# A graph layer on one core: VectorE normalises the second row tile and a small turn order at the end is changed

## What is computed

```python
h = relu(layernorm(x))                      # per row
xn = batchnorm(h) * norm1_g + norm1_b       # per column
agg = segment_sum(xn[src], dst) / max(deg, 1)
conv_out = relu(agg @ W_conv + b_conv)
q, k, v = heads(h_dense, Wq), heads(h_dense, Wk), heads(h_dense, Wv)   # the first 256 rows, 8 heads
attn = linear_attention(phi(q), phi(k), v)  # random features with exp
h_attn = (attn @ Wo)[pos]                   # rows past 255 take the last row
y = conv_out + h_attn + h
out = x + batchnorm(y) * norm2_g + norm2_b
```

## Time and profile before

| What | Value |
|---|---|
| Median of three executions | 176.18 us (175.99 to 176.76) |
| Profiled execution, its time | 176.07 us |
| Profiled execution, its span | 174.2 us |
| PE busy | 165.6 us (95%) |
| DVE busy | 137.9 us (79%) |
| ACT busy | 89.9 us (52%) |
| HBM read / written | 10.92 MB / 2.56 MB |

### The profile page before, as it was taken

How to read it: one execution, slowest core, us unless ns; L and a number is a source line. 1 busy time by engine, 2 the same in 40 slices (tenths; PEclk the granted TensorE clock), 3 DMA queues, 4 the chain that set the end, 5 groups by cost and what they waited for, 6 DMA issues and landing times.

```text
span 174.2 us, 3024 instructions
## 1 busy us (share of the span) xinstructions
PE 165.6 (95%) x1131; PEld 108.9 (63%) x1132; DVE 137.9 (79%) x315; ACT 89.9 (52%) x163; POOL 7.6 (4%) x22
## 2 busy tenths in 40 slices
PE   7899999999999999999999999999999999999960
PEld 2388877545545546557777798684464574767940
DVE  2868889989947786999656785975999998597981
ACT  3426999839694779979416164217600505004050
POOL 5037000000000000000000000000000000000000
PEclk9999999999999999999999999999999999999998
DMA  5997970000610000000000000000294014050046
GB/s 186 362 328 185 346 261 0 0 4 0 218 43 0 4 0 0 0 4 2 0 4 0 0 4 0 0 4 4 70 336 186 0 28 119 6 147 0 4 124 172
DMA packets 11884, 13.71 MB, mean 79 GB/s; under 512 B 1458, under 2 KB 6748, under 8 KB 11868
## 3 DMA queue, kind: packets, MB, share of 16 engines
q1 hardware_dynamic: 10476, 12.13, 21.3%
q10 hardware_dynamic: 1072, 1.10, 1.8%
q0 software_dynamic: 320, 0.26, 0.7%
HBM read 10.92 MB, written 2.56 MB: 77 GB/s over the span
## 4 chain that ended last, share of the span: by engine, by line
PE 88%; DVE 3%; ACT 3%; DMA 2%; issue 1%; DVEq 0%; ACTq 0%
PE bank L978 24%; PE bank L708 20%; PE bank L638 8%; PE bank L659 4%; PE bank L732 4%; PE bank L722 4%; PE bank L751 4%; PE bank L685 4%; PE bank L650 3%; PE bank L630 3%; PE bank L1005 2%; PE bank L696 2%; DMA xs<-in_x 2%; DVE gl L1222 1%; DVE st L1054 1%
## 5 line engine op out<-in xcount | busy, mean ns | idle before, releaser
L978 PE MATMUL bank<-r,gh 128*128 128x512 f16 (+8 forms) x140 | 39.3, 314 | 0.0
L978 PE MATMUL bank<-r,gl 128*128 128x512 f16 (+8 forms) x140 | 39.3, 313 | 0.0
L708 PE MATMUL bank<-wc,xs 128*128 128x512 f32 (+1 forms) x80 | 38.5, 608 | 0.2 <-DVE gl L1222 0.2
L1085 DVE TENSOR_TENSOR ohb<-iota,bcol 128x1280 f16<-128x1280 f16 x25 | 20.5, 818 | 3.7 <-PE bank L650 3.7
L708 PEld LDWEIGHTS bank<-wc,xs 128*128 128x128 f32 (+1 forms) x80 | 13.6, 187 | 11.6 <-issue 11.6
L392 ACT ACTIVATE r<-bank 128x500 f16<-128x500 f32 x25 | 18.3, 764 | 3.4 <-PE bank L650 3.4
L978 PEld LDWEIGHTS bank<-r,gh 128*128 128x128 f16 (+1 forms) x140 | 13.5, 97 | 8.5 <-issue 0.3
L978 PEld LDWEIGHTS bank<-r,gl 128*128 128x128 f16 (+1 forms) x140 | 13.6, 97 | 8.2
L608 ACT ACTIVATE bw<-mv,epst 128x1 f32<-128x1 f32 x4 | 1.2, 295 | 31.0 <-DVE mv L1385 31.0
L638 PE MATMUL bank<-hT,r 128*128 128x256 f32 x64 | 14.5, 381 | 0.0
L650 PEld LDWEIGHTS bank<-ohv,ohb 128*128 128x128 f16 x250 | 9.7, 98 | 6.7 <-issue 5.3
(11 more groups left out here) (177 smaller groups left out, 267.1 us busy)
## 6 DMA issues: line engine op xcount, KB each, us to landing
xs<-in_x SPq DMA_DIRECT2D x15, 256.0 KB, 4.6
out<-xs SPq DMA_DIRECT2D x7, 256.0 KB
r<-in_L_gnn_Wq SPq DMA_DIRECT2D x1, 1024.0 KB, 7.5
r<-in_L_gnn_Wk SPq DMA_DIRECT2D x1, 1024.0 KB, 5.7
wc<-in_L_gnn_W_conv SPq DMA_DIRECT2D x1, 1024.0 KB, 9.1
wvo<-in_L_gnn_Wv SPq DMA_DIRECT2D x1, 1024.0 KB, 11.2
wvo<-in_L_gnn_Wo SPq DMA_DIRECT2D x1, 1024.0 KB, 5.3
xs<-in_x ACTq DMA_DIRECT2D x3, 256.0 KB, 4.2
```

Of the source, the lines that this page charges most:

```text
L708: last = nc.tensor.matmul(acc[0:n, :], xnT[:, f, i * P:i * P + n], wc[:, f, :], start=(f == 0), stop=(f == FT - 1))
L978: last = nc.tensor.matmul(acc[:, 0:cn], gg[0:n, s, f * P:(f + 1) * P], A16[0:n, s, c0:c0 + cn], start=(s == 0 and gg is gh), stop=(s == NT ...
L1085: last = V.tensor_tensor(oh[:, s0:s0 + n, :].rearrange("p s (m t) -> p s m t", t=2), iota16[:, 0:size].rearrange("p (m t) -> p m t", t=2). ...
```

## The change

1. **Opening.** PE turns tile 1 first, then tile 0. Tile 1 is scaled and shifted by VectorE (`normal_second`, one instruction, without ReLU; a new semaphore `n1_ready`), and ACT's copy of the turned tile applies the ReLU. Tile 0 stays with ACT.
2. **Edge search in two parts.** Thresholds for 2 of 10 dst columns are made before `ln_scale(0)`, the other 8 after `normal_second`. PE counts the first part before the tiles are turned and the second behind one `rouse` matmul, where three stood. The parts stand in separate columns, and `first_rows` has one linked instruction more.
3. **Statistics.** Those of tiles 3 and 5 go ahead of `first_rows`, those of 2 and 4 stay behind.
4. **Loads.** W_q comes in halves of 256 columns, each with a semaphore, tiles 2 and 4 between them. W_k waits for tile 7, not 9.
5. **ACT** copies the first half of q before the square root of tiles 6 to 9.
6. **Feature tile 2.** Block 2, like block 0, is turned with x and copied by ACT; block 1 is turned last. VectorE's addition for block 2 goes.
7. **Feature tile 3.** VectorE normalises block 0, ACT block 1 in two pieces and block 2.
8. **Stores.** SP writes feature tile 2 in the order 0, 2, 1, and both transfers of feature tile 3's block 2; ACT issues that of block 1 alone.

```diff
-        order = [("hT", 0), ("hT", 1), ("first",), ("q", 0), ("q", 1), ("hT", 2), ("hT", 3), ("hT", 4), ("hT", 5),
+        order = [("first",), ("hT", 1), ("hT", 0), ("q", 0), ("q", 1), ("hT", 2), ("hT", 3), ("hT", 4), ("hT", 5),
...
-            sp.dma_start(wq, w_q.rearrange("(t p) n -> p t n", p=P)).then_inc(wq_in, 16)
-            for i in (2, 4, 6, 7, 8, 9):
+            sp.dma_start(wq[:, :, 0:2 * P], wq_rows[:, :, 0:2 * P]).then_inc(wq_in[0], 16)
+            load_x(2)
+            load_x(4)
+            sp.dma_start(wq[:, :, 2 * P:D], wq_rows[:, :, 2 * P:D]).then_inc(wq_in[1], 16)
+            for i in (6, 7, 8, 9):
...
-            sp.wait_ge(x_in[NT - 1], 16)
+            sp.wait_ge(x_in[7], 16)
...
-                for j in {FT - 2: (2, 0, 1), FT - 1: (0, 2)}.get(f, (0, 1, 2)):
+                for j in {FT - 2: (0, 2, 1), FT - 1: (0, 2)}.get(f, (0, 1, 2)):
...
-                        for i in range(8, NT if f < FT - 1 else 9):
+                        for i in range(8, NT):
...
             ln_tile(0)
-            ln_tile(1)
+            store_hT(1, ACT.Relu)
             store_hT(0)
-            store_hT(1)
...
+            qk_copy(0, 0)
             ln_std_of(2)
-            qk_copy(0, 0)
...
                     copy_turned(f - 1, 0)
+                    copy_turned(f - 1, 2)
                 act.wait_ge(st2_ready, f + 1)
-                for a, b in ((0, 512), (512, 1024), (1024, N)) if f < FT - 1 else ((0, 256), (256, 512), (1024, N)):
+                for a, b in ((0, 512), (512, 1024), (1024, N)) if f < FT - 1 else ((512, 768), (768, 1024), (1024, N)):
...
-            stored(act, "zT", FT - 1, 2)
-            act.dma_start(out[(NT - 1) * P:N, c], xs[0:LAST, NT - 1, c]).then_inc(o_out, 16)
...
             rouse(ROUSE)
+            edge_search(0)
             pe.wait_ge(id_set, 1)
+            transpose_h(1)
             transpose_h(0)
-            transpose_h(1)
-            edge_search()
-            rouse(ROUSE_MORE)
+            rouse(ROUSE_NEXT)
+            edge_search(1)
...
-            transpose_z(FT - 2, (1, 2))
             turn_with_residual(FT - 2, 0)
+            turn_with_residual(FT - 2, 2)
+            transpose_z(FT - 2, (1,))
             transpose_z(FT - 1)
...
+            def normal_second():
+                dve.wait_ge(ln_ready, 1)
+                V.tensor_scalar(xs[:, 1, :], xs[:, 1, :], lnw[:, 2, 1:2], lnw[:, 3, 1:2], ALU.mult, ALU.add).then_inc(n1_ready, 1)
...
+            edge_thresholds(0, SEARCHED)
             ln_scale(0)
-            edge_thresholds()
+            normal_second()
+            edge_thresholds(SEARCHED, EJ // GR)
+            ln_stats(3)
+            ln_stats(5)
             first_rows()
...
-                finish(f - 1, 2)
                 scale(f)
                 dve.wait_ge(st2_ready, FT)
-                V.tensor_scalar(yT[:, f, 512:1024], yT[:, f, 512:1024], s2[:, f:f + 1], t2[:, f:f + 1],
+                V.tensor_scalar(yT[:, f, 0:512], yT[:, f, 0:512], s2[:, f:f + 1], t2[:, f:f + 1],
```

More of the change, by code:

```diff
@@ L118, in gnn_kernel @@
         edst2 = r2[0:EP, 1280:1280 + EJ // GR].bitcast(F16).rearrange("p (j t) -> p j t", t=2)
-        first = sb("first", [P, 2], F32)
+        first = sb("first", [P, 4], F32)
         rows = sb("rows", [P, 2], I32)
@@ L201, in gnn_kernel @@
             order_end += [("agg", f, 0), ("agg", f, 1)] + [("zT", f - 1, j) for j in range(3)] + [("agg", f, 2)]
-        order_end += [("agg", FT - 1, c) for c in range(len(LAST_CHUNKS))] + [("zT", FT - 2, j) for j in (1, 2, 0)]
+        order_end += [("agg", FT - 1, c) for c in range(len(LAST_CHUNKS))] + [("zT", FT - 2, j) for j in (0, 2, 1)]
         order_end += [("zT", FT - 1, j) for j in range(3)]
@@ L248, in gnn_kernel @@
         pj_in = sem("pj_in")
-        wq_in = sem("wq_in")
+        wq_in = [sem(f"wq_in{i}") for i in range(2)]
         wk_in = sem("wk_in")
@@ L378, in _, with store_hT @@
         def _(act):
-            def store_hT(i):
+            def store_hT(i, func=ACT.Copy):
                 n = rows_of(i)
@@ L383, in store_hT @@
                 act.activation(hT[:, :, i * P:i * P + n], acc[:, :].rearrange("p (t n) -> p t n", t=FT)[:, :, 0:n],
[L384 removed]
+                               func).then_inc(read("hT", i), 1)
             stores = [0]
@@ L790, in rouse, with edge_search @@
                     nc.tensor.matmul(bank[0][:, :], cone[:, :], cone[:, 0:1].to_broadcast([P, 512]), start=True, stop=True)
-            def edge_search():
-                pe.wait_ge(nb_ready, 1)
-                acc = pe_open(pe, "first")
-                for hf in range(2):
[L796 to L799, removed]
+            def edge_search(part):
+                pe.wait_ge(nb_ready, part + 1)
+                if part == 0:
+                    pe_open(pe, "first")
+                acc = bank[uses[("first",)][0]]
+                a, b = ((0, SEARCHED), (SEARCHED, EJ // GR))[part]
+                for hf in range(2):
+                    for j in range(a, b):
+                        last = nc.tensor.matmul(acc[0:GROWS, 2 * part + hf:2 * part + hf + 1],
+                                                below[:, j, hf * GROWS:(hf + 1) * GROWS], cone[0:EP, 0:1],
+                                                start=(j == a), stop=(j == b - 1))
+                if part:
+                    last.then_inc(full("first"), 1)
             def project_consts():
@@ L984, in turn_with_residual @@
                 pe.wait_ge(z_act, 3 * f + j + 1)
-                for i in range(4 * j, 4 * j + 4):
+                for i in range(4 * j, min(4 * j + 4, NT)):
+                    n = rows_of(i)
                     pe.wait_ge(x_in[i], 32)
@@ L988, in turn_with_residual @@
                     nc.tensor.matmul(acc[:, o:o + P], yT[:, f, i * P:(i + 1) * P], ident[:, :], start=True, stop=False)
-                    last = nc.tensor.matmul(acc[:, o:o + P], ident[:, :], xs[:, i, f * P:(f + 1) * P], start=False, stop=True)
+                    last = nc.tensor.matmul(acc[:, o:o + P], ident[0:n, :], xs[0:n, i, f * P:(f + 1) * P], start=False, stop=True)
                 last.then_inc(full("zT", f, j), 1)
@@ L1046, in _, with ln_stats, ln_moments @@
             V.memset(cone[:, :], 1.0).then_inc(dve_cst, 1)
[L1048 to L1056, removed]
+            def ln_stats(i):
+                if i == NT - 1:
+                    dve.wait_ge(pad_zero, 1)
+                dve.wait_ge(x_in[i], 16)
+                return V.bn_stats(st[:, i, :], xs[:, i, :])
+            def ln_moments(gi):
+                for i in range(*LN_GROUPS[gi]):
                     ins = V.bn_aggr(mv[:, i, :], st[:, i, :])
```

49 lines of the change are left out of this document (33 added, 16 removed).

## The result

The changed kernel takes 175.46 us (median of 12 executions, 174.70 to 176.16), the kernel before 176.15 (12, on the same chip in turn). The ratio is 0.9948 [0.9932, 0.9964]: **0.9 us faster**, where 1.28 was forecast. The two medians lie 0.69 apart. The profiled execution took 174.95 with a span of 173.1; it was forecast at 174.8 with 172.94.

What follows compares the result with a forecast made beforehand. PE, busy 95% of the span, was taken as the bound, so edits pay ahead of its gapless run or behind it. Opening 0.86 plus end 0.40 gave 1.26 us: a median of 174.9 us, range 174.2 to 175.8.

Steps and rivals of the forecast that it cites:

- Turns start, behind VectorE: Opening: PE starts turning tiles at 7.75, after VectorE's normalised tile 1, 0.19 us sooner.
- Turns' end to W_q: Opening, PE's list: 0.67 of 1.78 us goes, as two matmuls on constants and 4 of 20 search matmuls leave.
- Products with W_q: Opening: these products start at 10.13 instead of 10.99, 0.86 us sooner, a gain expected to reach the last phase whole.
- Loads: Opening: W_q in halves makes smaller row pieces that could cost speed; put at 0, with 0.5 us as upper end.
- Constants' cover: Opening: matmuls on constants and the early search finish before the turns start, with 0.13 us to spare, against 0.56 before.
- Stall at W_k: First products with W_k, near 19.1 us: PE waits for neither a PSUM bank nor the load; put at 0.
- Block 0 added, from aggregation's start: End, feature tile 3: VectorE's addition for block 0 starts at 167.42 against 168.81, the opening's gain included.
- End's data: End, stores: the last data ends at 171.64, without a hole in the DMA engines' work; the end gains 0.40 us.
- End in the span: End: the span ends 1.30 us behind the last data, at 172.94 instead of 174.2; the end's part is 0.40.
- the sign that was to prove the opening wrong: Opening: a PE wait for VectorE or for a load before 20 us in the new profile.
- the rival that it gains nothing: End: slower writes, or ACT's second copy and added turns delaying block 1, leave no gain; 175.3 us, chance 0.12.
- The clock rival: Opening: PE falls to 1.2 GHz, and 16 of 32 W_q passes cost 0.22 more each; 178.4 us, chance 0.05.

Runs made afterwards that it cites:

- e3: The changed kernel with 15 instead of 18 matmuls on constants at the start; 175.90 us, ratio 0.9969 to the kernel before.
- e1: The kernel before with only the opening part of the change (points 1 to 5), the end as before; 175.50 us, ratio 0.9943.
- e4: The changed kernel measured again without an edit; 175.53 us, ratio 0.9960 to the kernel before.
- g1: f2's kernel with W_k's load waiting for tile 6 instead of tile 7; 175.49 us, ratio 0.9947 to the kernel before.
- g3: The changed kernel with 21 instead of 18 matmuls on constants at the start; 175.84 us, ratio 0.9975 to the kernel before.
- f4: The changed kernel with tile 1 left to ACT and the turns in the old order; 175.74 us, ratio 0.9982 to the kernel before.
- f3: The changed kernel with the old load order: W_q whole ahead of tiles 2 and 4, W_k behind tile 9; 175.51 us, ratio 0.9992.
- f1: The changed kernel with 15 full matmuls on constants plus three of one column, instead of 18 full ones; 175.23 us, ratio 0.9945.
- g4: The changed kernel with 15 matmuls on constants and the last small store issued by ACT; 175.77 us, ratio 0.9969.
- f2: The changed kernel with feature tile 3's last store (row tile 9) issued by ACT as before, not SP; 175.33 us, ratio 0.9950.
- g2: Feature tile 2's block 2 turned plainly and added by VectorE, as before, the rest as in the changed kernel; 175.83 us, ratio 0.9972.
- e2: The kernel before with only the new end (points 6 to 8), the opening as before; 176.67 us, ratio 1.0004.

## Why the prediction came out as it did

| Step | Forecast | Measured |
|---|---|---|
| Turns start, behind VectorE | 7.75, -0.19 | 7.70 (e3) to 7.91 (e1) behind VectorE; behind constants in the profiles after, e4, g1 and g3; worth 0.29 with the tiles' order (f4) |
| Turns end | 9.02 (7.75 and 1.27) | 8.88; 8.97 in e1 |
| Turns' end to W_q | 1.11, -0.67 | 1.78 to 1.09, -0.69 |
| Products with W_q | 10.13, -0.86 | 9.97; 9.72 to 10.06 over the eleven profiles with this opening |
| Loads | 0, at most 0.5 lost | 0.5 of mean span **gained** (f3), 0.2 of median |
| Constants' cover | 0.13, no wait | used up in some executions, costs about 0.2 (e3, f1, g4) |
| Stall at W_k | 0 | 0 in the profile after, up to 0.2 in others |
| Block 0 added, from aggregation's start | -0.54 | 49.33 to 48.87, -0.47 |
| End's data | -0.40 | -0.3 |
| End in the span | -0.40 | about -0.2 |
| Clock falls | 0.05 | didn't |
| Time | 174.9, -1.28 | 175.46; -0.9 by the ratio, -0.69 by the medians |

**The opening was right in its steps.** In the profile after, the aggregation starts at 118.57 where it was 119.47, -0.90; in e1's, with the late tile 0 of x, at 118.80, -0.67. Across executions e1's span is 0.87 (within 0.26) below that of the kernel before in its batch (173.69 against 174.56). That this meets the 0.86 so well is in part luck. The medians of the two are only 0.65 apart; the rest of the mean is the long executions, which hardly occur with the new order of loads and for which the sum had nothing. The terms that were off made up for each other: the loads, put at 0, gave something, and so did the shorter turns, while the constants and, in some executions, W_k took something. The prediction looked at one profile, in which tile 2 (7.7) held up nothing, and couldn't see that other executions have it late. The largest term, the 0.67 between the turns and W_q, is read from the profiles alone: no run undoes the split search or puts the two matmuls back. And the sign that was to prove the opening wrong, a PE wait for a load before 20 us, is absent from the profile after but there, small, in f1, f2 and g2.

**The end was mis-sized.** The step that failed is the last one, from the addition to the span's end. The additions moved nearly as forecast. Measured from the start of the aggregation, block 0's addition comes 49.34 (before) and 49.33 (e1) later with the old end, and 48.87 with the new one in the profiles after, e4, f2 and f3: -0.47. The DMA view of 168 to 176 us, in 40 slices of 0.2 us (share in tenths), shows where the data ends with the old end, before and in e1:

```profile
DMA  0599989999706989999999871000000000000000
```

```profile
DMA  9989999319999999999851000000000000000000
```

That is 172.8 and 172.1, 53.3 behind the aggregation's start in both. With the new end it is 171.6 in the profile after and 171.5 in f2 (its line stands further down), 53.0 behind it: 0.3 sooner, and not 0.40. The old end has a hole of 0.3, the 0 at 170.2 and the 3 and 1 at 169.4 to 169.8. The forecast let it vanish, but the new end has one of 0.2, at 168.0 to 168.2 in f2's line. Then comes the tail. It was taken as 1.30 from a window that ended at 172.90, past the data; it is 1.4 before, 1.6 in e1 and 1.5 to 1.7 with the new end. So the span's end comes 54.73 (before) and 54.9 (e1) behind the aggregation's start, and 54.53 (after), 54.61 (e4) and 54.64 (f2) with the new end: 0.1 to 0.2 sooner than before, 0.3 to 0.4 sooner than e1. Why the tail differs is open. Span means put the end at 0.20 (within 0.22), 173.49 with the new end against 173.69 without (e1), and e2 at 0.10 (within 0.38).

**And part of this may not reach the time.** The prediction took 1.87 us outside the span as fixed. It is that in 92 of 92 executions of the kernel before (1.76 to 1.95) and in 11 of 11 of e1. With the new end it was 1.94 and 2.07 on average in the two measurements of the changed kernel and 1.88 in f2, 0.09 (within 0.08) more over the three. What is left of the end is about 0.1: the rival that it gains nothing is nearer to what was measured than the forecast's 0.40. e1 and e2 point the same way, but neither interval shuts out 0.40 by itself.

**Whether it is faster** hangs on the measure: the prediction wanted more than 0.5%, below 175.3. The ratio is just past 0.5%, the median of 175.46 isn't.

**The clock rival** failed as the trace of before suggested. From 7.77 to 9.97 PE had 20 matmuls of one column, eight turns and one full matmul, and the 32 passes behind them took 7.02, 0.22 each, at the higher level (2.4 GHz); so in every profile. How many passes a fall would have slowed (16 in the prediction) no run shows. The Trainium skill (TensorE: Matmul & The Clock Gate, Part 4: PE-mode transpose) says that turns don't count as work for the clock in the same way; if that holds, this stretch of 2.2 us, mostly turns and single columns, did not bring it down here.

## What to carry to other kernels

A gain ahead of a gapless run of the bounding engine arrived nearly whole here (0.65 by medians, 0.87 by means, of 0.86); a gain at the end is only worth what the stores' queue lets through, so sum it on the DMA engines and on the tail behind them. Where a load's landing differs from one execution to the next, move it ahead even if the one profile has it covered, and judge it by the mean span of many executions. And compare time, span and the difference of the two for each variant, since an edit can shorten the span and lengthen what is outside.

## What the runs showed that was not expected

**Time outside the span.** It is 1.8 to 1.95 us, or, in some executions of some kernels, up to 3.0, mostly above 2.3 (the changed kernel has two just under it, 2.24 and 2.27). In five profiles with the long one (e2, e3, f1, g3, g4) a last transfer of the instruction queue comes after the last data. The DMA view of 168 to 176 us, in 40 slices of 0.2 us (share in tenths, GB/s), first e3 (2.45 outside), then f2 (1.9):

```profile
DMA  8199999999999999992000000000000000300000
GB/s 195 54 282 292 248 300 300 271 256 328 279 282 330 269 287 266 203 228 69 23 21 3 0 0 0 0 0 0 0 0 0 0 0 0 82 0 0 0 0 0
```

```profile
DMA  2899999999999999830000000000000000000000
GB/s 54 269 289 264 279 313 274 241 335 292 279 320 271 282 274 210 220 87 23 21 8 0 0 0 0 0 0 0 0 0 0 0 0 0 0 0 0 0 0 0
```

The DMA view of e3 from 174.6 to 175.2 names it:

```profile
DMA packets 1, 0.02 MB, mean 27 GB/s; under 512 B 0, under 2 KB 0, under 8 KB 0
...
q8 instruction: 1, 0.02, 10.6%
```

It starts at 175.0, 1.7 us behind the span's end; in f2 its like started at 165.3. But g1 has it late too (174.7) and had 1.96 outside, so it goes with the long time and doesn't explain it alone. Which edit brings it on is open: it never came with the old end (0 of 103 executions, before and e1), often with 15 constants (17 of 24), seldom with 18 (2 of 36 in the changed kernel and f2), with 21 in 5 of 12, and keeping the code's length (f1) left it in one of six. The constants can't be all of it: e2, with the old opening and the new end, has it in 5 of 12.

**PE's step from 1.2 to 2.4 GHz** came at times from 3.75 to 7.14 us in the profiles, behind the same list of constants from 1.21 on. Covers of a tenth of a microsecond behind such a list mean nothing.

**A branch on PE** (0.32 to 0.84 us of "issue") and the landing of the same transfer (6.4 to 7.6 us, with the same queue ahead of it) differ from one execution to the next by more than most of the terms of this prediction.
